# The dynamic convolution of a four-layer kernel: the last copy of a sample between the pieces of the next ones, the first expert on ScalarE, and the first mixing ahead of the second input

## The reference, cut to what matters

```python
g = jnp.mean(x, axis=(2, 3))                       # x is already normalised
h = jax.nn.relu(g @ w1.T + b1)
alpha = jax.nn.softmax(h @ w2.T + b2, axis=-1)     # 4 numbers a sample
weff = jnp.einsum('bk,koihw->boihw', alpha, experts)
out = conv3x3(x, weff) + beff                      # per sample
```

## Time and profile before

| what | value |
|---|---|
| median of 3 executions | 3130.79 us (3127.74 to 3137.73) |
| the profiled execution's own time | 3132.45 us |
| its span in the trace | 3130.7 us |
| the stage dyn_conv | 0 to about 429 us of it |
| 204 to 228 us: busy PE, DVE, ACT, POOL | 20.31, 20.54, 17.28, 4.67 us of 24 |
| mean granted TensorE clock there | 0.93 of full |

### The profile page before, as it was taken

How to read it: one execution, slowest core, us unless ns; L and a number is a source line. 1 busy time by engine, 2 the same in 40 slices (tenths; PEclk the granted TensorE clock), 3 DMA queues, 4 the chain that set the end, 5 groups by cost and what they waited for, 6 DMA issues and landing times. The chain is left out here.

```text
span 3130.7 us, 71818 instructions
## 1 busy us (share of the span) xinstructions
PE 2747.3 (88%) x25712; PEld 2482.8 (79%) x25712; DVE 2172.1 (69%) x5174; ACT 1363.0 (44%) x2113; POOL 288.4 (9%) x801
## 2 busy tenths in 40 slices
PE   5888879999999999917969998878999999999791
PEld 3666669999999999913447777758999999999791
DVE  7888846666666666687018888886666666666865
ACT  3766642246632222236436666643225662222120
POOL 1112110000000000045000101010000000000602
PEclk9899989999999999958979999998999999999795
DMA  4334230000000000087054877856000000000758
GB/s 89 81 90 99 67 124 0 0 0 0 0 0 0 0 0 0 0 233 198 1 87 73 120 104 102 116 73 107 0 0 0 0 0 0 0 0 0 121 94 127
DMA packets 735622, 164.89 MB, mean 53 GB/s; under 512 B 728209, under 2 KB 728849, under 8 KB 730641
## 3 DMA queue, kind: packets, MB, share of 16 engines
q1 hardware_dynamic: 608928, 136.86, 22.7%
q10 hardware_dynamic: 126576, 26.41, 5.4%
HBM read 96.13 MB, written 67.11 MB: 52 GB/s over the span
## 5 line engine op out<-in xcount | busy, mean ns | idle before, releaser
L269 PE MATMUL L_conv<-L_x_hi,L_w_hi 128*128 128x256 f32 x5040 | 1251.0, 283 | 46.5 <-DVE L_w_lo L236 28.7
L269 PE MATMUL L_conv<-L_x_hi,L_w_lo 128*128 128x256 f32 x5040 | 1249.5, 283 | 0.0
L156 ACT ACTIVATE L_row_b<-S,L_bias 128x256 f32 (+1 forms) x1008 | 514.2, 510 | 1168.9 <-DVE L_x_hi L210 1158.0
L269 PEld LDWEIGHTS L_conv<-L_x_hi,L_w_hi 128*128 128x128 f32 x5040 | 958.7, 190 | 49.5 <-issue 28.9
L269 PEld LDWEIGHTS L_conv<-L_x_hi,L_w_lo 128*128 128x128 f32 x5040 | 957.0, 190 | 0.0
L220 DVE SCALAR_TENSOR_TENSOR S<-L_conv,L_neg_bias,L_row_b 128x256 f32 x1008 | 487.7, 484 | 517.5 <-PE L_conv L273 516.7
L273 PE MATMUL L_conv<-L_x_lo,L_w_hi 128*128 128x256 f32 x5040 | 771.3, 284 | 4.9 <-DVE L_x_lo L212 4.8
L273 PEld LDWEIGHTS L_conv<-L_x_lo,L_w_hi 128*128 128x128 f32 x5040 | 677.7, 190 | 7.4 <-DVE L_x_lo L212 7.4
L212 DVE TENSOR_TENSOR L_x_lo<-S,L_x_hi 128x256 fp32r<-128x256 f32 x1016 | 455.3, 448 | 34.7
L210 DVE TENSOR_SCALAR L_x_hi<-S 128x256 fp32r (+1 forms) x1016 | 316.7, 312 | 35.3
L604 PE MATMUL dc_conv<-dc_xz_hi,dc_w_hi 128*128 128x512 f32 x384 | 171.3, 446 | 6.5 <-DVE dc_w_lo L731 6.5
(11 more groups left out here) (177 smaller groups left out, 2896.4 us busy)
## 6 DMA issues: line engine op xcount, KB each, us to landing
dc_raw<-x SPq DMA_DIRECT2D x32, 512.0 KB, 6.6
x_scratch<-dc_raw SPq DMA_DIRECT2D x16, 1024.0 KB, 7.4
lp_xr<-x_scratch SPq DMA_DIRECT2D x16, 1024.0 KB, 7.0
x_scratch<-lp_xr SPq DMA_DIRECT2D x32, 512.0 KB, 7.7
at_res<-x_scratch SPq DMA_DIRECT2D x32, 512.0 KB, 10.5
x_scratch<-at_res SPq DMA_DIRECT2D x64, 256.0 KB, 5.3
fs_buf<-x_scratch SPq DMA_DIRECT2D x32, 512.0 KB, 6.7
at_G<-x_scratch ACTq DMA_DIRECT2D x56, 256.0 KB, 5.8
```

What stands on the lines that cost most here:

```text
L156: nc.scalar.activation(row_b[p][:, :, :], line(k, at_step(k, i), p), ACT.Identity, bias=bias[:, k:k + 1]).then_inc(row_b_ready[p], 1)
L269: nc.tensor.matmul(out, w[:, k, s * P:(s + 1) * P], x_hi[p][:, s:s + J, :], start=(s == 0 and n == 0), stop=False)
```

## The change

Three moves of work inside `dyn_conv`.

1. `to_slot` is now one instruction a call. Of a sample's four moves, three stand where four did in the next sample (two after high_weights, one after chunk 2's evacuation), and the fourth, (1,1), goes into the sample after that, between the evacuation of chunk 3 and `centre(n+1, 0)`.
2. The product of the first expert with its factor goes from VectorE to ScalarE (`first_expert`). With it `centre(n+1, 1)` stands ahead of `exps`, and on VectorE `remainder(n+1, 1)` goes from behind chunk 1's statistics to ahead of `mix` e = 1.
3. Ahead of sample 0, the mixing and low_weights come right after the softmax; both remainders and the statistics of sample 1 follow. The experts are loaded from SyncE's queue right behind sample 0. In sample 0, TensorE's `group(1, INP)` stands behind chunk 1, `hid(1)` behind chunk 2 and `logits(1)` inside chunk 3. At the end VectorE makes three of sample 15's moves and ScalarE one.

```diff
-PER_LOOP = 34
+PER_LOOP = 32
@@ SyncE
-            for n in range(PER):
+            load(0, 0)
+            sp.dma_start(ex[0], halves(experts[:, 0, :])).then_inc(ex_in, 16)
+            sp.dma_start(ex_rest[:, :, :], experts[:, 1:KE, :]).then_inc(ex_in, 16)
+            for n in range(1, PER):
                 load(n, n)
@@ ScalarE
-            act.dma_start(ex[0], halves(experts[:, 0, :])).then_inc(ex_in, 16)
-            act.dma_start(ex_rest[:, :, :], experts[:, 1:KE, :]).then_inc(ex_in, 16)
+            def first_expert(m):
+                act.wait_ge(weight_ready, m + 1)
+                nc.scalar.activation(w_mix, ex[0], ACT.Identity, scale=weight[:, 0:1]).then_inc(first_mixed, 1)
...
-            def to_slot(n, u, ph):
+            def to_slot(n, u, ph, pw):
                 act.wait_ge(affine_ready, n + 1)
-                for pw in range(2):
-                    dst, src, scale, shift = slot_move(n, u, u % 2, ph, pw)
-                    nc.scalar.activation(dst, src, ACT.Identity, bias=shift, scale=scale).then_inc(s_done, 1)
+                dst, src, scale, shift = slot_move(n, u, u % 2, ph, pw)
+                nc.scalar.activation(dst, src, ACT.Identity, bias=shift, scale=scale).then_inc(s_done, 1)
...
                 if not first:
                     evacuate(n * CH - 1, (k - 1) % PER, CH - 1, n - 1)
+                if not first and not second:
+                    to_slot(n - 2, (k - 2) % PER, 1, 1)
                 if not last:
                     centre(t, k + 1, 0)
                 evacuate(n * CH, k % PER, 0, n)
                 if not last:
                     hidden(n + 1)
+                    centre(t, k + 1, 1)
                     exps(n + 1)
-                    centre(t, k + 1, 1)
+                    first_expert(n + 1)
                 evacuate(n * CH + 1, k % PER, 1, n)
                 if not last:
                     high_weights(n + 1, (k + 1) % 2)
                 if not first:
-                    to_slot(n - 1, (k - 1) % PER, 0)
+                    to_slot(n - 1, (k - 1) % PER, 0, 0)
+                    to_slot(n - 1, (k - 1) % PER, 0, 1)
                 evacuate(n * CH + 2, k % PER, 2, n)
                 if not first:
-                    to_slot(n - 1, (k - 1) % PER, 1)
+                    to_slot(n - 1, (k - 1) % PER, 1, 0)
...
             evacuate(B * CH - 1, B % PER - 1, CH - 1, B - 1)
-            to_slot(B - 1, (B - 1) % PER, 0)
+            to_slot(B - 2, (B - 2) % PER, 1, 1)
+            to_slot(B - 1, (B - 1) % PER, 0, 0)
@@ TensorE, sample 0 only
+                if first:
+                    for q in range(2):
+                        products_high(0, q, 0, 0)
+                        products_high(0, q, 0, 1)
+                        products_low(0, q, 0)
+                    group(1, INP)
...
@@ VectorE
-                chain.step(nc.vector.tensor_scalar(weight, prob, total, inp_affine[:, 0:1], ALU.mult, ALU.mult))
+                nc.vector.tensor_scalar(weight, prob, total, inp_affine[:, 0:1], ALU.mult, ALU.mult).then_inc(weight_ready, 1)
...
-                if e == 0:
-                    chain.step(nc.vector.tensor_scalar(w_mix, ex[0], weight[:, 0:1], None, ALU.mult))
-                else:
-                    chain.step(nc.vector.scalar_tensor_tensor(out=w_mix, in0=ex[e], scalar=weight[:, e:e + 1],
-                                                              in1=w_mix, op0=ALU.mult, op1=ALU.add))
+                if e == 1:
+                    dve.wait_ge(first_mixed, m + 1)
+                chain.step(nc.vector.scalar_tensor_tensor(out=w_mix, in0=ex[e], scalar=weight[:, e:e + 1],
+                                                          in1=w_mix, op0=ALU.mult, op1=ALU.add))
...
                     mixing_weights(n + 1)
-                    for e in range(KE):
+                    remainder(n + 1, k + 1, 1)
+                    for e in range(1, KE):
                         mix(n + 1, (k + 1) % 2, e)
                 if not first:
                     result_affine(n - 1, k - 1)
                 result_stats(n * CH + 1, k % PER, 1)
                 if not last:
-                    remainder(n + 1, k + 1, 1)
                     low_weights(n + 1, (k + 1) % 2)
...
-            remainder(0, 0, 0)
             softmax_in(0)
-            remainder(0, 0, 1)
+            mixing_weights(0)
+            dve.wait_ge(ex_in, 2 * 16)
+            for e in range(1, KE):
+                mix(0, 0, e)
+            low_weights(0, 0)
+            for z in range(2):
+                remainder(0, 0, z)
             for q in range(CH):
                 input_stats(0, 1, q)
             aggregate("input", INP)
             squares(INP)
-            mixing_weights(0)
-            dve.wait_ge(ex_in, 2 * 16)
-            for e in range(KE):
-                mix(0, 0, e)
-            low_weights(0, 0)
...
-            for pw in range(2):
-                dst, src, scale, shift = slot_move(B - 1, (B - 1) % PER, (B - 1) % 2, 1, pw)
+            for ph, pw in ((0, 1), (1, 0), (1, 1)):
+                dst, src, scale, shift = slot_move(B - 1, (B - 1) % PER, (B - 1) % 2, ph, pw)
                 nc.vector.tensor_scalar(dst, src, scale, shift, ALU.mult, ALU.add)
```

More of the change, by code:

```diff
@@ L408, in dyn_conv @@
     w_mixed, w_hi_ready, w_ready = sem("w_mixed"), sem("w_hi_ready"), sem("w_ready")
+    weight_ready, first_mixed = sem("weight_ready"), sem("first_mixed")
     me_ready, group_done, var_ready, rstd_ready = ([sem(f"{kind}_{x}") for kind in ("res", "inp")]
@@ L555, in sample @@
                 first, last = isinstance(n, int) and n == 0, isinstance(n, int) and n == B - 1
+                second = isinstance(n, int) and n == 1
                 if not first:
                     evacuate(n * CH - 1, (k - 1) % PER, CH - 1, n - 1)
+                if not first and not second:
+                    to_slot(n - 2, (k - 2) % PER, 1, 1)
                 if not last:
@@ L576, in _ @@
             centre(0, 0, 0)
-            centre(0, 0, 1)
             hidden(0)
             exps(0)
+            act.wait_ge(ex_in, 2 * 16)
+            first_expert(0)
+            centre(0, 0, 1)
             high_weights(0, 0)
@@ L625, in sample @@
                 first, last = isinstance(n, int) and n == 0, isinstance(n, int) and n == B - 1
+                if first:
[4 more added lines that the diff above has]
+                    group(1, INP)
+                    products_high(0, 2, 0, 0)
+                    products_high(0, 2, 0, 1)
+                    products_low(0, 2, 0)
+                    hid(1)
+                    products_high(0, 3, 0, 0)
+                    logits(1)
+                    products_high(0, 3, 0, 1)
+                    products_low(0, 3, 0)
+                    return
                 if not last:
@@ L633, in sample @@
                 products_high(n, 1, u, 0)
-                if not first:
-                    group(n - 1, RES)
+                group(n - 1, RES)
                 if not last:
```

## The result

The changed kernel takes 3141.74 us (median of 11 runs, 3135.92 to 3146.15), the one before 3130.15 us in the same comparison (11 runs, 3126.49 to 3137.73). The ratio is 1.0034, with a 95% interval of 1.0026 to 1.0042: slower by 11.6 us, where +12.1 was forecast.

A forecast was written before the change was run, and what follows sets the result against it. A loop bounds the kernel: ScalarE from high_weights to centre (13.18 us) plus VectorE from remainder 0 to the additions (10.43), 23.61 a sample. 12.7 + 2.6 - 3.0 - 0.7 + 0.5 = +12.1 on 3130.8: 3143 us, 8-in-10 range 3134 to 3155.

The forecast's parts named there:

- The fourth move: Delayed move ahead of centre: ScalarE's part +0.16 us to 13.34; VectorE's 1.7 us wait goes but is spent at remainder 0.
- The first expert and remainder 1: VectorE's part: product leaves (1.05 us), remainder 1 enters (2.48 us), +1.25 us to 11.68; ScalarE's product 0.95 us, hidden.
- The 13 periods: High_weights of the second sample to the last: 11 undisturbed at 25.02 us, two at 25.2, plus 2.0: 327.6 us, +12.7.
- small hesitations: Remainder of the 13 periods beyond the summed parts: 4.0 us before, half kept, 2.0.
- the two turns: Periods holding a turn of the loop, where VectorE stands 2.33 us: 13.5 + 11.68 = 25.2 us, against about 25.6 before.
- The start: Ahead of the loop: TensorE starts 8.3 us earlier, but group(1)'s copy comes at 38.8 instead of 35.97: +2.6 us.
- The end: Samples 14 and 15: chunk 3 evacuated one move earlier, so sample 15's last evacuation comes earlier: -3.0 us.
- The last moves: End of the stage: ScalarE's two moves take 4.24 us, VectorE's three 3.5: -0.7 us.
- a late TensorE: Allowance in the sum for TensorE coming late at times: 0.5 us.
- VectorE as the pace: Rival: VectorE paces the loop, period 23.0 us, 3122 us; needs ScalarE's part under 11.3 us; chance 0.11.
- TensorE as the pace: Rival: TensorE, standing some 4.6 us ahead of logits, decides; period grows by 1.4 us, 3161 us; chance 0.09.
- hardly any change: Rival: start keeps its head start (+0.2), hesitations vanish (-2), remainder costs 1.0 not 1.25 (-2.8): 3135 us; chance 0.17.

The follow-up runs named there:

- e1: Changed kernel with remainder 1 back behind the statistics of chunk 1, first expert still on ScalarE: 3123.08 us, ratio 0.9972.
- e2: Changed kernel with remainder 1 back behind the statistics, the first expert back on VectorE and exps ahead of centre 1: 3127.35 us, ratio 0.9986.
- e3: Changed kernel with the fourth move back in its old place behind the third: 3148.41 us, ratio 1.0051.
- e6: Changed kernel with the fourth move behind centre(n+1, 0) instead of ahead of it: 3118.11 us, ratio 0.9956.
- e5: Kernel with mixing as before and the changed moves and start, plus the fourth move put behind centre(n+1, 0): 3125.86 us, ratio 0.998.
- e7: Changed kernel with remainder 1 behind the mixing, fourth move behind centre, and sample 0's group(1) inside chunk 1: 3118.08 us, ratio 0.9947.
- e8: Changed kernel with only TensorE's order of sample 0 altered, group(1) behind 24 products instead of 36: 3139.32 us, ratio 1.0017.
- e4: Kernel before with only the start changed, mixing and moves (the last ones too) as before: 3134.45 us, ratio 1.0005.
- e9: Changed kernel with the fourth move behind centre 0 and sample 0's group(1) behind 24 products: 3117.29 us, ratio 0.9943.

## Why the prediction was right

**What bounds the kernel.** Shown. The undisturbed period followed the sum of the two engines' parts through six different orders: 23.61 before, 25.03 after, 23.65 (e1), 23.77 (e2), 24.9 (e3), 23.05 (e6), each within 0.2 us of the one expected. In e6 the part ahead of remainder 0 is no longer ScalarE's but runs over VectorE's statistics, group and GpSimd to gate_mean. In e5 and e7 three and five of the 13 periods do not follow it.

**The fourth move.** +0.16 us was forecast for ScalarE's part, measured 13.28 - 13.18 = +0.10 in the samples shown; over all undisturbed samples it is 13.26 to 13.37 against 13.17 to 13.21, about +0.13, and e3 gives the same. That VectorE would spend at remainder 0 what it gained was right (2.13 us there); that its wait for chunk 3's evacuation would go was wrong: 1.1 of its 1.7 us are left, and 0.8 at chunk 2's came in. Both are off the loop, so this changed nothing.

**The first expert and remainder 1.** +1.25 us a period forecast, measured 11.75 - 10.43 = +1.32. ScalarE's product was put at 0.95 and took 0.91. Uncovered it is worth 0.12 us an undisturbed period (e1 against e2), as the 0.1 named. The Trainium skill, "ScalarE: Activation LUTs", What ACT_TABLE_LOAD costs, gave an estimated 0.92, with which this trace's 0.91 agrees. The advice of its Rules for kernel authors, to keep plain multiplication on VectorE, did not hold for this one, by those 0.12 us; the page gives its reason for bf16, and this product is fp32.

**The 13 periods.** +12.7 forecast, +13.35 measured. Right in sum, by two errors that cancel in part: the small hesitations all but vanished (2.0 kept), and the two turns took 26.2 instead of 25.2. The failed step is the turn: the working followed gate_mean to remainder 0 (13.57 us from H, 13.5 forecast) and forgot TensorE's hid, which waits for gate_mean too and stood 3.8 us. Behind it the products ran at the lower clock, group(RES) and logits were late, and VectorE's part took 12.64 us instead of 11.74.

**The start.** +2.6 forecast; high_weights of sample 2 came 3.67 us later. The mechanism (group(1) behind 36 products) is shown by e8, and the head start's loss by e4. The term was 1 us too small: the copy came at 39.24 and not at 38.8, and the way on from it took 0.4 us more, not 0.2 less.

**The end.** -3.0 forecast with bounds of -1.5 and -3.3, measured from H of sample 15 to chunk 3's last evacuation: 428.71 - 405.89 = 22.82 against 27.67, **-4.85**. This is the term that was mis-sized. It took the 13.4 us of 48 products for fixed. They took 11.9 (416.44 to 428.36): group(14, RES) no longer stood 2.53 us ahead of them, and the granted clock was at its upper level throughout. Another 0.65 us came from group(14, RES) at H + 10.55, where 11.2 was taken. The last moves gave -0.7 as said: 3.53 against 4.24.

Sum of the measured terms: 3.7 + 13.35 - 4.85 - 0.7 = 11.5, against 11.4 at the stage's end; forecast 12.1 with 0.5 for a late TensorE. That the total came within 0.5 us is in part luck: start and periods were put 1.7 us too small together, the gain at the end 1.85 us too small, and the 0.5 us for a late TensorE did not come on top.

**The rivals.** VectorE as the pace did not happen, and e6 shows that it starts where it was said to. TensorE as the pace did not happen in the changed kernel: with 46.8 us of standing at hid and logits its undisturbed periods still are 25.0 to 25.1, but for the first, 25.3. I had put that stand wholly at logits; part of it is at hid. Of the three conditions of hardly any change one came true, as the hesitations fell from 4.0 to about 0.7 us; the start kept none of its head start, and the remainder cost 1.32 us and not 1.0.

**Open.** Why the identity lands late in 3 of 10 traces that load the experts on SyncE's queue is only argued: it is the last of the transfers on ScalarE's queue, and the experts' 1.5 MB now run beside it. The order of two issues goes with it: SyncE issued the 1152 KB of experts 0.05 and 0.01 us ahead of the identity in e3 and e5, 0.06 us behind it in e9, and 0.17 to 0.89 us behind it in the seven others. No run sets this order on purpose, so it is a lead and no cause. The kernel before has one trace with the identity in time, so whether the change made the delay more frequent was not tested.

## What to carry to other kernels

When no engine is full, look for the loop through two of them: start at an instruction that waits with its engine idle, and add up what stands between it and the next such one; here work moved into that stretch was paid in full, and work moved about outside it changed no undisturbed period. Covering another engine's 0.9 us with 2.5 us of one's own work is a loss when that work was off the loop before: first ask where the filler stood. And a head start on one engine is worth only what the next shared point lets through; here 8.5 us were gone at the first tiny product that stood behind 36 large ones, and with 24 ahead of it (e8) VectorE's moved work was over no sooner.

## What was not expected of the hardware

The same 48 products took 13.4 us after a stand of 2.53 us and 11.9 with no wait ahead of their group (416.44 in the rows above). The windows of the kernel before show the granted clock behind that stand (columns as in the windows above):

```profile
401.60:403.00 1.40, 1.31 (x5) 1.12 (x6) 0.76 (x6) 0.12 (x1) 0.00 (x0) 0.61 1.04 427
403.00:404.50 1.50, 1.50 (x5) 1.21 (x4) 0.81 (x3) 0.00 (x0) 0.86 (x5) 0.50 0.01 0
404.50:406.00 1.50, 1.50 (x6) 1.16 (x6) 0.00 (x0) 0.00 (x0) 1.06 (x6) 0.73 0.00 0
```

and those of the changed kernel at the same place of its sample:

```profile
416.40:419.00 2.60, 2.57 (x13) 2.13 (x13) 1.54 (x7) 1.01 (x2) 0.71 (x4) 1.00 0.53 214
```

In the kernel before the granted clock was 1.00 again from 406.0 to 407.5 us, with TensorE busy all the while, and the 1.5 us are what the stand cost on top of itself. A turn of VectorE's loop costs 2.33 to 2.41 us for which the profile names no wait, the same in both kernels. A small transfer of 64 KB landed 4.6 to 9.7 us after its issue in otherwise equal starts.
